# Graph attention kernel: the sum of two weighted rows, from an accumulating transfer to a GpSimd instruction

## The reference

```
src = concat(edge_src, arange(N));  dst = concat(edge_dst, arange(N))   # 10000 edges + a loop on each node
xl = x @ Wl + bl;  xr = x @ Wr + br
e = leaky_relu(xl[src] + xr[dst], 0.2);  logits = sum_c e * att        # per edge and head
p = exp(logits - max over the edges with the same dst)
out[dst] = sum(p * xl[src]) / sum(p) + bias
```

## Time and profile before

| | |
|---|---|
| median of 3 runs | 3177.54 us |
| the profiled execution: its own time | 3172.86 us |
| its span | 3171.1 us |
| busy: PE / DVE / ACT / POOL | 2669.1 / 2662.8 / 1689.2 / 1200.7 us |
| first edge pass: first gather, last L706 | 541.83 us, 1046.79 us |
| L657 (POOL multiply), x160, mean | 1282 ns |
| L652 (the accumulating transfer, as POOL issues it), x160, mean | 967 ns |
| L644, L646 (gathers, as POOL issues them), x160 each, mean | 1078 ns, 1524 ns |
| L817 (DVE), x128, mean | 939 ns |
| bytes moved on POOL's queue in the whole program | 202.14 MB |

### The profile page before, as it was taken

How to read it: one execution, slowest core, us unless ns; L and a number is a source line. 1 busy time by engine, 2 the same in 40 slices (tenths; PEclk the granted TensorE clock), 3 DMA queues, 4 the chain that set the end, 5 groups by cost and what they waited for, 6 DMA issues and landing times. The chain is left out here.

```text
span 3171.1 us, 41550 instructions
## 1 busy us (share of the span) xinstructions
PE 2669.1 (84%) x11205; PEld 1815.5 (57%) x11205; DVE 2662.8 (84%) x5834; ACT 1689.2 (53%) x4291; POOL 1200.7 (38%) x1061
## 2 busy tenths in 40 slices
PE   7999997988885299999988878825999999688886
PEld 5777775433332188888843333303888888455554
DVE  7989996899999376667759999967888885599999
ACT  3545553467667333333316767665788886244443
POOL 0022211788885233333348888823333331000000
PEclk8999998999998599999989999966999999799998
DMA  8989997688886488888758888848999995488886
GB/s 322 340 304 318 319 342 291 185 225 221 224 222 169 148 282 275 270 265 265 247 188 215 220 227 221 222 110 338 358 353 349 345 349 194 170 288 291 293 289 224
DMA packets 355220, 830.73 MB, mean 262 GB/s; under 512 B 57630, under 2 KB 58176, under 8 KB 344778
## 3 DMA queue, kind: packets, MB, share of 16 engines
q1 hardware_dynamic: 265464, 622.14, 56.1%
q0 software_dynamic: 87072, 202.14, 25.3%
q10 hardware_dynamic: 2452, 3.79, 0.4%
HBM read 510.62 MB, written 329.28 MB: 265 GB/s over the span
## 5 line engine op out<-in xcount | busy, mean ns | idle before, releaser
L890 PE MATMUL bank<-wr,nT_e 128*128 128x512 f32 x1280 | 614.2, 625 | 29.5 <-DVE z_e L749 29.2
L1047 PE MATMUL bank<-whi,t_hi 128*128 128x512 f32 x1256 | 524.0, 417 | 24.0 <-DVE t_lo L408 24.0
L1048 PE MATMUL bank<-wlo,t_hi 128*128 128x512 f32 x1256 | 499.6, 398 | 0.0
L1049 PE MATMUL bank<-whi,t_lo 128*128 128x512 f32 x1256 | 498.1, 397 | 0.0
L890 PEld LDWEIGHTS bank<-wr,nT_e 128*128 128x128 f32 x1280 | 243.9, 201 | 290.8 <-issue 290.5
L914 POOL DMA_INDIRECT g_vin<-touched,node_slot x157 | 175.9, 1120 | 325.6 <-DMA g_xin<-in_x 293.7
L914 POOL DMA_INDIRECT vin<-touched,node_slot x157 | 170.9, 1088 | 337.4 <-DMA vin<-rows 328.9
L693 ACT ACTIVATE w_e<-vs_e,ex_e 128x128 f32<-128x128 f32 x640 | 204.4, 390 | 167.2 <-DVE acc_e L817 112.2
L1047 PEld LDWEIGHTS bank<-whi,t_hi 128*128 128x128 f32 x1256 | 237.9, 189 | 75.6 <-issue 17.5
L1049 PEld LDWEIGHTS bank<-whi,t_lo 128*128 128x128 f32 x1256 | 237.2, 189 | 58.5
L986 ACT CAST t_hi<-bank 128x512 fp32r<-128x512 f32 (+1 forms) x157 | 91.8, 585 | 330.1 <-PE bank L1049 329.9
(11 more groups left out here) (245 smaller groups left out, 6256.0 us busy)
## 6 DMA issues: line engine op xcount, KB each, us to landing
rows<-t_row SPq DMA_DIRECT2D x312, 512.0 KB, 4.4
w_e<-w_e POOLq DMA_DIRECT2D x160, 256.0 KB
touched<-done_e SPq DMA_DIRECT2D x160, 256.0 KB
xin<-in_x SPq DMA_DIRECT2D x156, 256.0 KB, 4.6
xTin<-in_xT SPq DMA_DIRECT2D x156, 256.0 KB
vin<-rows SPq DMA_DIRECT2D x156, 256.0 KB, 4.0
g_vin<-rows SPq DMA_DIRECT2D x156, 256.0 KB
g_xin<-in_x SPq DMA_DIRECT2D x156, 256.0 KB
```

The source lines that it names most:

```text
L890: pe.matmul(psR[b][:, :], nT[:, b, cc, :], wr[:, cc, :], start=(cc == 0), stop=False)
L1047: pe.matmul(ps, hi[:, cc, :], whi[:, cc, :], start=(cc == 0), stop=False)
L1048: pe.matmul(ps, hi[:, cc, :], wlo[:, cc, :], start=False, stop=False)
L1049: last = pe.matmul(ps, lo[:, cc, :], whi[:, cc, :], start=False, stop=(cc == KC - 1))
```

## The change

The semaphores `w_added` (one per buffer, counted by transfers) are replaced by one semaphore `added`. `add_own` no longer issues a transfer that reads `w2` and adds it into `w1` on the DMA engines; instead POOL adds `w2` to `w1` itself with one `tensor_tensor` of 128x512. `accumulate` waits for `added` to reach t + 1.

```diff
-        g["w_added"] = [ctx.enter_context(nc.semaphore(f"w_added{u}")) for u in range(WR)]
...
-                  "bottom exps cap ups left_over inverted weighted summed scaled trail_set trail_stored others_loaded "
+                  "bottom exps cap ups left_over inverted weighted added summed scaled trail_set trail_stored others_loaded "
...
-        w_added, w0 = g["w_added"], layer * 16 * len(range(0, T, WR))
...
             def add_own(t):
                 b = t % WR
                 pool.wait_ge(s["weighted"], t + 1)
-                pool.dma_start(w1[:, b, :], w2[:, b, :], accum_op=ALU.add).then_inc(w_added[b], 16)
+                pool.tensor_tensor(w1[:, b, :], w1[:, b, :], w2[:, b, :], ALU.add).then_inc(s["added"], 1)
...
             def accumulate(t):
                 i, b = t // G, t % WR
-                dve.wait_ge(w_added[b], w0 + 16 * (t // WR + 1))
+                dve.wait_ge(s["added"], t + 1)
                 need(dve, s["scaled"], t - AR + 1)
```

## The result

The changed kernel takes 3259.82 us (median of 4 runs, 3259.12 to 3261.92) against 3176.69 us before (median of 4): ratio 1.0266, 95% interval 1.0246 to 1.0286. One of the four runs before, 4519.93 us, was a slow one; it counts in the median and not in the ratio. The changed kernel is 83 us slower; 3272 was forecast. The profiled execution took 3259.12 us, 86 us more than the profiled one before.

The account below looks back on a forecast made before the run. DVE was taken to bound the kernel, its busy time partly waits for POOL's elementwise instructions. 3172.9 us plus 103 (28.5 periods x 3.62) minus 3.5 in the tails gave 3272 us, range 3225 to 3335.

Parts of the forecast that it names:

- The bound: Edge passes: DVE, busy 59.31 of 60 us, sets the pace; the accumulating transfer is hidden and less traffic is worth nothing.
- POOL busier: Sign in the busy times that would show the forecast: DVE still 98% busy and POOL busier than its 50.03 of 60 us.
- The price of the add: POOL's add right behind its multiply L657: likeliest cost to DVE is the whole second instruction, 1.21 us per in-phase tile.
- in-phase tile: Edge-pass tile where POOL's multiply L657 starts 0.17 us after L765; five together take 27.05 us, and 33.10 with the add.
- POOL keeps its turn: Handover between POOL's multiply and add: the add goes before waiting DVE; 3250 to 3290 us, chance 0.45.
- first rival: DVE gets its turn between POOL's multiply and add: period 32.6 us, +88 us, total 3257 us; chance 0.22.
- POOL stays in phase: POOL's multiply, add and two gathers fit the 6.05 us plain tile, so the next multiply is on time, 0.3 us to spare.
- Today's 29.48: Period of five edge-pass tiles before the change, three of them out of phase by a held gather at 0.8 us each.
- the hold of the gathers: POOL's gather issue takes 0.98 us, but 1.79 begun inside L754 and 1.44 begun in L759, held by that DVE instruction.
- The rival by which gathers are not held: A gather issue always costs 0.98 us: period 31.8 us, +66 us, total 3235 us; chance 0.05.
- the term of -3.5 us: Tail of each pass: ACT's 1.74 us of idle time before its last group goes, -3.5 us for both passes.

Follow-up runs that it names:

- write_only: The changed kernel with POOL's add replaced by a fill of zeros to a 128x1024 scratch tile, the sum left out: 3173.20 us, ratio 0.9994.
- no_add: The sum of the two weighted rows left out, with neither the transfer of the kernel before nor the add: 3110.32 us, ratio 0.9798.
- moved_before: The kernel before, transfer kept, with accumulate moved behind pair_sums in DVE's stream: 3182.71 us, ratio 1.0024.

## Why the prediction was right, and where it was not

**The bound** held. DVE is full before and after (59.31 and 59.45 of 60 us), DVE had waited for the transfer only 5.1 us, and with part of the traffic brought back the time stayed. "POOL busier", a sign that the prediction named, did not come: 44.26 us in place of 50.03, since POOL waits for DVE more.

**The price of the add, 1.21 us per tile on DVE through its second SBUF operand,** held in kind, as L815 and L776 beside the add and the fill of `write_only` show. In the size, tile by tile, it did not. The prediction let each in-phase tile grow by 1.21. Against the in-phase tiles (`no_add`) the growth was 1.06 with `peaks`, 1.00 with `sums_up`, 1.02 with L820, 0 in one plain tile and 2.14 in the other. Together 5.2 instead of 6.05.

**"POOL keeps its turn"** is the step that failed. I drew it from one row, L780 in the earlier trace rows, and applied it to all tiles. It is so only where POOL arrives without idle time. In the four tiles of a period in which POOL has waited for DVE, DVE's first two-operand instruction is served after the multiply, as in my first rival; that rival's plain tile of 4.84 is exactly there, and so are its long ones, L778 and L803 (L776 with 1.19 us and L801 with 1.17 here). But its late plain tile (5.78) isn't: there POOL kept its turn, and it cost 6.98. Nor is its tile with L822, 7.38 by its sum and 6.30 measured. The period is 32.31, a little under the rival's 32.6 and under my 33.10. That both sums come so near is in part luck: my plain tiles, 6.05 and 6.05, were 1.22 too long and 0.93 too short, and in the rival's the errors of the two tiles just named, 1.20 too short and 1.08 too long, cancel.

**"POOL stays in phase"** failed with it. The add waits for L815 in the in-phase tile, the next gather begins inside L757 and is held (1.37 us), and the following multiply is late by 0.9 us. It recovers in the tiles with L820 and the chains, as before.

**Today's 29.48 and the hold of the gathers** were read rightly: `no_add` gives 27.11 where I had worked out 27.05. The rival by which gathers are not held is out: 2.84 us in `moved_before`. The page SBUF of the Trainium skill (State Buffer; who interferes with whom, the practical consequences) infers that a `tensor_tensor` on VectorE doesn't stall descriptor generation. For these gathers the measurement differs and decides: one that began inside the `tensor_tensor` L759 took 1.44 us instead of 0.98.

**The tail** lost its idle time as forecast, 1.74 us in the first pass and 0.76 in the second, where less had been there, but the term of -3.5 us did not come. From the last leaky instruction to the cast L716 (L714) behind ACT's last group it was 34.5 and 33.6 us before, and is 34.0 and 34.0: nothing in sum. The idle time went, and ACT got to its last groups later by as much.

## What to carry to other kernels

Before moving work to GpSimd, count the SBUF operands on VectorE. Here a GpSimd multiply or add of 128x512 held two-operand VectorE instructions until it had ended, even one of four elements per partition, and a one-operand copy too; the busy share hides it, since the wait counts as busy. Compare min and max of a line's duration to find it. And an engine that is not the bound still sets the phase: here one issue of 1.28 us per tile cost 65 us, and half as many issues gave 31 of them back.

## What the runs showed of the hardware

- Of two elementwise GpSimd instructions in a row: after the first, a waiting two-operand VectorE instruction is served if GpSimd had been idle before the pair (asked 0.96 to 2.04 us after its start), and not if it came straight from a gather (asked 0.04 to 1.13 us after). A gather followed at once by one elementwise instruction holds VectorE in the same way (1.85 to 1.95 us), from some 0.3 us after the gather's start: 81 of 81, against 0 of 722 beside other gathers.
- A fill on GpSimd, 128x1024 floats in 0.96 us, holds no two-operand VectorE instruction.
- A gather's issue, 0.95 to 0.98 us undisturbed, took 2.84 us when three two-operand VectorE instructions stood in a row.
- A one-operand copy on VectorE (L812, 128x512, SBUF to SBUF) is held too: 0.41 us long in the kernel before (L814), 2.74 and 2.72 beside the pair, once in each pass.
